# Attention values of two steps issued together in every four steps of a one-core attention and channel-mix kernel

## What is computed

```
x = x + layernorm(attention(layernorm(x)))      # 16 heads of 16, 1024 keys, softmax, output projection
x = x + layernorm(ffn(layernorm(x)))            # channel mix
attention: softmax(q k^T * 0.25) v, then @ w_o.T
ffn:       xr, xk = mixes of x and x shifted by one token
           out = sigmoid(xr @ W_r.T) * (relu(xk @ W_k.T)^2 @ W_v.T)
```

## Time and profile before

| | before |
|---|---|
| runs | 1274.4 us median (1273.76 to 1274.73) |
| profiled execution | 1274.69 us, span 1272.9 us |
| TensorE busy | 1252.4 us, 98% of the span |
| ScalarE busy | 1067.7 us, 84% |
| VectorE busy | 779.1 us, 61% |
| GpSimd busy | 276.4 us, 22% |
| granted TensorE clock | 0.998 of full speed |

### The profile page before, as it was taken

How to read it: one execution, slowest core, us unless ns; L and a number is a source line. 1 busy time by engine, 2 the same in 40 slices (tenths; PEclk the granted TensorE clock), 3 DMA queues, 4 the chain that set the end, 5 groups by cost and what they waited for, 6 DMA issues and landing times.

```text
span 1272.9 us, 25486 instructions
## 1 busy us (share of the span) xinstructions
PE 1252.4 (98%) x10604; PEld 603.3 (47%) x10604; DVE 779.1 (61%) x1725; ACT 1067.7 (84%) x1159; POOL 276.4 (22%) x356
## 2 busy tenths in 40 slices
PE   8999999999999999999999999999999999999997
PEld 5544454454544444454544544444444445534344
DVE  6543747758465773847567584666747466463737
ACT  4788888888888888888888888888888888898872
POOL 3000212222211321222121221223222122222211
PEclk9999999999999999999999999999999999999999
DMA  4455553317712194124733166321871129400001
GB/s 153 115 144 166 98 129 78 101 51 126 124 52 84 52 180 87 52 66 106 144 68 113 42 116 125 73 84 51 143 124 51 35 75 174 85 1 20 15 1 34
DMA packets 61797, 112.70 MB, mean 89 GB/s; under 512 B 6512, under 2 KB 31344, under 8 KB 61616
## 3 DMA queue, kind: packets, MB, share of 16 engines
q1 hardware_dynamic: 61360, 109.60, 38.8%
q10 hardware_dynamic: 288, 1.05, 0.3%
HBM read 68.42 MB, written 41.94 MB: 87 GB/s over the span
## 4 chain that ended last, share of the span: by engine, by line
PE 93%; DVE 3%; ACT 2%; DMA 1%; POOL 0%; issue 0%; ACTq 0%; DVEq 0%
PE O L602 38%; PE S L583 26%; PE M L353 14%; PE M L340 11%; PE M L250 3%; ACT PT L590 1%; DVE sth L701 1%; DMA A<-w_dram 1%; PE M L483 1%; DVE A L710 0%; PE S L1016 0%; POOL rsh L706 0%; DVE QS L474 0%; ACT QS L471 0%; DVE A L914 0%
## 5 line engine op out<-in xcount | busy, mean ns | idle before, releaser
L590 ACT ACTIVATE PT<-S 128x1024 f32<-128x1024 f32 x1024 | 1003.5, 1026 | 156.8 <-PE S L583 156.2
L602 PE MATMUL O<-PT,V 128*17 128x512 f32 x4096 | 538.9, 598 | 0.0
L583 PE MATMUL S<-QS,KS 50*128 50x512 f32 x2048 | 465.4, 450 | 3.2 <-ACT PT L590 3.2
L583 PEld LDWEIGHTS S<-QS,KS 50*128 50x128 f32 x2048 | 211.0, 183 | 452.7 <-ACT PT L590 375.2
L602 PEld LDWEIGHTS O<-PT,V 128*17 128x17 f32 x4096 | 67.8, 95 | 139.5 <-issue 137.7
L705 POOL TENSOR_SCALAR veh<-mvh 128x2 f32<-128x2 f32 x96 | 22.3, 232 | 491.3 <-DVE mvh L703 490.1
L914 DVE SCALAR_TENSOR_TENSOR A<-Z,M 128x512 f32<-128x512 f32 x30 | 20.4, 682 | 159.6 <-PE M L353 159.6
L340 PE MATMUL M<-xnT,WH 64*128 64x512 f32 (+1 forms) x504 | 110.7, 393 | 1.1 <-DVE WL L985 1.1
L353 PE MATMUL M<-WH,xnT 64*128 64x256 f32 (+1 forms) x496 | 83.0, 278 | 0.0
L353 PE MATMUL M<-WH,cT 64*128 64x256 f32 (+1 forms) x496 | 82.1, 278 | 0.5 <-DVE rec L661 0.4
L353 PE MATMUL M<-WH,C 64*128 64x256 f32 (+1 forms) x496 | 81.8, 278 | 0.0
(11 more groups left out here) (130 smaller groups left out, 1610.0 us busy)
## 6 DMA issues: line engine op xcount, KB each, us to landing
scr<-p SPq DMA_DIRECT2D x124, 256.0 KB
QS<-scr SPq DMA_DIRECT2D x56, 256.0 KB, 6.7
KS<-scr SPq DMA_DIRECT2D x56, 256.0 KB, 11.0
QS<-scr SPq DMA_DIRECT2D x70, 128.0 KB, 6.0
KS<-scr SPq DMA_DIRECT2D x68, 128.0 KB, 8.5
xA<-x_dram SPq DMA_DIRECT2D x16, 512.0 KB, 7.0
xB<-x_dram SPq DMA_DIRECT2D x16, 512.0 KB, 7.2
out_dram<-xB SPq DMA_DIRECT2D x15, 512.0 KB, 3.4
```

Source lines behind the costliest of these rows:

```text
L583: fn = lambda e, p=p, a=a, rows=rows: e.matmul(PS[p][:, a, :], KS[qd][rows, p, kt * 128:kt * 128 + 128], QS[qd][rows, p, hf * 512:hf * 512 ...
L590: e_fn = lambda e, p=p: e.activation(PT[i % 2][:, 2 * p:2 * p + 2, :], PS[p][:, :, :], ACT.Exp, scale=SCALE)
L602: fn = lambda e, j=j: e.matmul(PO[32 * j:32 * j + 17, :], V[b % 2][:, kt, 4 * qd + j, :], PT[i % 2][:, j, :], start=(kt == 0), stop=(kt == 7))
```

## The change

Outside the last batch and the first 12 steps, steps are taken in fours (s % 4). In step 0 two rounds are pumped, one between the scores pairs and one behind them, and its values are held back. In step 1 there is one round, and the values of steps 0 and 1 stand one behind the other. In step 2 nothing is pumped: the second scores pair follows the first at once. Step 3 is as before. A bank is taken only two steps behind its release, and only one turn may begin in a step. `PT` has three buffers in place of two, paid for with one of the two `T` buffers.

```diff
-        T = [sb(f"T{i}", [128, 512]) for i in range(2)]
+        T = sb("T", [128, 512])
...
-        PT = [sb(f"PT{i}", [128, 4, 512]) for i in range(2)]
+        PT = [sb(f"PT{i}", [128, 4, 512]) for i in range(3)]
...
-            banks = [k for k in range(3) if bank_free[k] is not None and step_now[0] >= freed_at[k] + age]
+            banks = [k for k in range(3) if bank_free[k] is not None and step_now[0] >= freed_at[k] + max(age, bank_age[0])]
...
+                    if isinstance(block, Turn) and last_turn[0] == step_now[0]:
+                        return None
                     if isinstance(block, Turn) and now[0] is not None and now[0].tokens == block.tokens is not None:
                         return None
+                    if isinstance(block, Turn) and paired[0]:
+                        last_turn[0] = step_now[0]
...
-                exp_of[i, p] = act.op(e_fn, s_of[i, p], pv_of.get(i - 2))
+                exp_of[i, p] = act.op(e_fn, s_of[i, p], pv_of.get(i - 3))
...
-                pump(0 if u == 0 and s < 9 else 32 - s, age, (lambda: scores(i + 1, 1)) if nxt else None)
-                values(i)
+                paired[0] = b + 1 < B and (u > 0 or s >= 12)
+                bank_age[0] = 2 * paired[0]
+                late = (lambda: scores(i + 1, 1)) if nxt else None
+                if not (paired[0] and s % 4 == 2):
+                    pump(0 if u == 0 and s < 9 else 32 - s, age, late)
+                    if paired[0] and s % 4 == 0:
+                        pump(32 - s, age)
+                elif late:
+                    late()
+                if paired[0] and s % 4 == 0:
+                    held.append(i)
+                else:
+                    for k in (*held, i):
+                        values(k)
+                    held.clear()
```

More of the change, by code:

```diff
@@ L158, in sandwich_kernel @@
         load_weights(sp, xb_flat[1], "wkf", "wvf")
-        load_weights(sp, T[0], "wr")
+        load_weights(sp, T, "wr")
         rows_of_quad = [None, None]
@@ L301, in step_part @@
                 until_rest(block.done(block.bank[0], PM[block.bank[0]], ends[1]))
-        doubled = [False]
+        paired = [False]
+        doubled, bank_age, last_turn = [False], [0], [-1]
         def pump(left, age=1, between=None):
@@ L589, in scores @@
                         s_of[i, p] = pe.op(fn)
-                e_fn = lambda e, p=p: e.activation(PT[i % 2][:, 2 * p:2 * p + 2, :], PS[p][:, :, :], ACT.Exp,
+                e_fn = lambda e, p=p: e.activation(PT[i % 3][:, 2 * p:2 * p + 2, :], PS[p][:, :, :], ACT.Exp,
                                                    scale=SCALE)
-                exp_of[i, p] = act.op(e_fn, s_of[i, p], pv_of.get(i - 2))
+                exp_of[i, p] = act.op(e_fn, s_of[i, p], pv_of.get(i - 3))
                 last_exp[p] = exp_of[i, p]
@@ L602, in values @@
                 fn = lambda e, j=j: e.matmul(PO[32 * j:32 * j + 17, :], V[b % 2][:, kt, 4 * qd + j, :],
-                                             PT[i % 2][:, j, :], start=(kt == 0), stop=(kt == 7))
+                                             PT[i % 3][:, j, :], start=(kt == 0), stop=(kt == 7))
                 if j < 3:
@@ L621, in quad @@
                 return
-            at, half = T[g % 2], qd % 2
+            at, half = T, qd % 2
             view = at[:, :].rearrange("p (y r) -> p y r", r=32)
@@ L626, in quad @@
             yield REST
-            d = dve.op(lambda e: e.transpose(at[:, :], On[:, :]), d, tk.get(("T", g % 2)), split_of["wr"])
+            d = dve.op(lambda e: e.transpose(at[:, :], On[:, :]), d, tk.get("T"), split_of["wr"])
             tk["On_read"] = d
@@ L632, in quad @@
                                                  ALU.mult), d, tk.get("CC_read"))
-            tk["rec_read"] = tk["T", g % 2] = d
+            tk["rec_read"] = tk["T"] = d
             if not half:
@@ L642, in quad @@
                                                     ALU.subtract), d)
-            tk["T", g % 2] = tk["cT", g // 4, qd // 2, 0] = tk["cT", g // 4, qd // 2, 1] = d
+            tk["T"] = tk["cT", g // 4, qd // 2, 0] = tk["cT", g // 4, qd // 2, 1] = d
         def last_quad(g, qd):
-            at, half, parts_of = T[g % 2], qd % 2, [{}, {}]
+            at, half, parts_of = T, qd % 2, [{}, {}]
             for h, got in enumerate(parts_of):
@@ L655, in turned @@
                 x = got["cols"]
-                got["T"] = dve.op(lambda e: e.transpose(at[:, x], On[:, x]), got["On"], tk.get(("T", g % 2)))
+                got["T"] = dve.op(lambda e: e.transpose(at[:, x], On[:, x]), got["On"], tk.get("T"))
             def divided(got):
@@ L1069, in sandwich_kernel @@
         split_weights(["wq", "wk"])
+        held = []
         for u in range(2 * B):
```

## The result

The changed kernel took **1338.84 us** (median of 4 runs, 1337.11 to 1339.77) against 1274.09 us (1273.76 to 1274.73) before: 1.0504 times as long, 95% interval 1.0491 to 1.0516. Slower was right. The loss was 64.8 us where 25 had been forecast, and the time lies above the range that ended at 1318. The profiled execution took 1337.11 us, its span is 1335.3 us.

The account below looks back on a forecast made before the run. TensorE, 98% busy, was taken to bound the kernel. Its own work falling 13.1 us and waits adding 38.2 gave +25.1, so 1299.5 us, slower by 2.0%; range 1266 to 1318.

Parts of the forecast that it names:

- TensorE's own work: Joints save 34.9 us, lone halves add 17.6, turns between scores pairs 4.2: 13.1 us less, 1.65 put on a batch.
- exponentials, with the copies of O: Scores pairs waiting for ScalarE where pairs adjoin, 1.9 us a batch; copies of O at group starts, 0.6.
- z0's turn: Turn late behind VectorE's statistics and norms after y1: 1.0 us a batch, bounds 0 and 1.5.
- the other unit's turn: Turn for the next batch waiting for a bank behind the same VectorE work: 0.9 us, same bounds as z0.
- first k block, odd unit: First k matmul after z0's turn, late behind the mix and GpSimd's second subtraction: 1.3 to 1.8 us, taken as 1.5.
- first k block, even unit: First k matmul of the other unit, behind the mix: late by 0.1 us a batch.
- waits taken to be there before: Waits the batch of the kernel before already holds: 0.3 us taken off 6.0, leaving 5.7.
- Waits for VectorE and GpSimd: Part of the prediction on z0's turn and the other unit's, together 1.9 us a batch, and the k blocks, 1.6.
- Faster: Rival: waits on VectorE and ScalarE are covered, under 1.9 us a batch, so 1261 us; chance 0.17.
- Slower still, by VectorE and GpSimd together: Rival: three more casts per batch stretched beside GpSimd's subtraction, adding 12 us, so 1311 us; chance 0.13.
- Weights bare: Rival: joined values pay 0.1 for weights, scores pairs between rounds stay 0.34; 11 + 18 us, 1328 us; chance 0.04.

Follow-up runs that it names:

- run 16: Not a follow-up run: in "they run 16 matmuls over all rows" it is a verb and a count, said of the joined values, 1.84 us.

## Why the prediction was wrong

By its own steps, in a batch, measured in the fifth from start to start:

| in a batch, us | predicted | measured |
|---|---|---|
| TensorE's own work | -1.65 | -0.3 |
| exponentials, with the copies of O | 2.5 | 1.5 |
| z0's turn | 1.0 | 1.3 |
| the other unit's turn | 0.9 | 1.0 |
| first k block, odd unit | 1.5 | 1.3 |
| first k block, even unit | 0.1 | 1.5 |
| y0 for `cT`, both units | not in the sum | 2.2 |
| stretch at half clock | not in the sum | 1.6 |
| waits taken to be there before | -0.3 | |
| sum | +4.05 | +10.1 |

The difference, 6 us a batch, over some six and a half batches is the 39 us by which the forecast fell short.

**The step that failed** is the part "Waits for VectorE and GpSimd". It looked for waits along the one chain that was tight before, y1 to z0 to k in the odd unit, and got each of them right to within 0.3 us. It gave the even unit's k 0.1 us, and never looked at y0. Both had about 1.4 us to spare before (686.85 - 685.39 for k, 649.53 - 648.12 for y0). For k I had taken that as cover against a tighter schedule. It was no cover against an exchange on VectorE, where pieces of 3 to 5 us in all move ahead of the awaited cast at y0, and against VectorE and GpSimd stretching each other in the new order. Together 3.6 of the 6 us. That the late chains end in GpSimd's subtractions is shown by taking them out (24.3 us off the changed kernel, 1.7 off the other), and the exchange at y0 by the two sets of rows above, with the odd unit's four 0 joined and not joined: its places change, and the wait of 0.7 us comes and goes. For the even unit's k the exchange is read from the rows and was not undone by a run. No run parts the exchange from the stretching. By the rows the stretching alone is 1.0 us at y0 in each unit (0.46 + 0.55 and 0.46 + 0.57) and 1.3 at k (0.91 + 0.41), so 3.4 us of a batch, about as much as the three waits in TensorE's rows (1.16, 0.69 and 1.34); in the old order these pieces ran alone. Why the joined four swaps the pieces was not followed through the code.

**A term that was mis-sized:** TensorE's own work. The joint saves 0.24, not 0.32, since the scores pair ahead of joined values takes 0.40. That is 1.3 us a batch. The lone halves came as reckoned: the rounds of a batch take 2.3 us more (25 x 0.70 in seven batches is 2.5). The waits for exponentials were put 1.0 us a batch too high, which by luck takes back most of this. Two slips in the working carry little: 13.1 us over seven batches is 1.9, not the 1.65 given for one, and 740.85 - 738.64 less 0.9 is 1.3, not 1.2.

**Not foreseen:** half clock for 3.4 us behind a wait, 1.6 us a batch.

**The rivals.** "Faster" fell with the list of waits: they come to 8.8 us a batch, where it needed less than 1.9. "Slower still, by VectorE and GpSimd together" had the right kind of mechanism, and a time of 1311. It had three casts of a batch stretched by 0.57 us, 1.7 in all, where the awaited chains held 3.4. It lacked the exchange, and said by the earlier trace rows that GpSimd's own 1.29 does not grow; here it grows to 1.66 and 1.70, and it had grown in the kernel before too, to 1.73 for `cT` at 685.75. The Trainium skill, "SBUF — State Buffer", "Who interferes with whom", says that a VectorE instruction in a two-port mode, or with two inputs in SBUF beside a GpSimd instruction that reads SBUF, excludes GpSimd's and is excluded by it for a whole instruction; the rows at wait 2 agree in that both engines' pieces get longer side by side. "Weights bare" fell in both halves: joined values without a gap, and 0.24 for a scores pair between two rounds. By the rule of the Trainium skill, "TensorE: Matmul & The Clock Gate", "What overlaps and what doesn't", a weight load overlaps running matmuls of other rows only; the joined values disagree, as they run 16 matmuls over all rows in 1.84 us, two times 0.87 and 0.1 to leave the column strips.

## What to carry to other kernels

When an edit shifts when pieces are issued on one engine, list for every block that waits what stands ahead of its last input on VectorE and GpSimd, in both orders. A change of places there can cost one or more whole instructions, and make pieces longer that ran alone before; spare time in the old trace is no cover against it. Ask of each awaited piece whether its own engine was busy or idle just before it: here GpSimd was idle, and the delay lay one engine further back. Where an edit saves a little in many places and waits in a few, time it place by place and keep it only where it pays: 32 of 109 joints gave 6 us, all of them together lost 65.

## What the runs showed that I had not expected

The granted clock fell to half in the middle of a busy kernel. In the changed kernel that was six stretches of 3.4 us, five of them right behind the z turn of the odd unit. There TensorE had stood idle for 1.2 us and then run eight transposes with four scores matmuls between them. The kernel before has none but at its very start and its very end. Each of the six stands behind a wait of 0.9 or 1.2 us at a turn, and filling the one ahead of the z turn took away the falls there. But a wait alone does not decide it: the sixth batch of the changed kernel has the same waits and no fall, the run with only the rounds moved has waits of 0.9 to 1.3 us and no fall, and the run without the subtractions has fewer waits and twelve falls. What decides stays open.
